# A decoder's expert weights leave one by one behind named cross-attention products instead of in one go

## What is computed

```python
x = _layernorm(x + _L1_attn_ref(x, w_qkv, w_o))
x = _layernorm(x + _L1_xattn_ref(x, ctx_2048, ctx_2048))
logits = x @ gate_w.T
topk_w, topk_idx = top_k(softmax(logits), 8)
for e in range(64):           # w13: 256x256, w2: 256x128 per expert
    h = silu(x @ w13[e, :128].T) * (x @ w13[e, 128:].T)
    acc += combine[:, e:e+1] * (h @ w2[e].T)
x = _layernorm(x + acc)
```

## Time and profile before

| | us |
|---|---|
| runs of the kernel | 808.4, 811.34, 811.78 (median 811.34) |
| profiled execution | 814.26 |
| its span | 812.9 |
| PE busy | 736.4 (91%) |
| DVE busy | 496.7 (61%) |
| POOL busy | 371.7 (46%) |
| ACT busy | 369.5 (45%) |

### The profile page before, as it was taken

How to read it: one execution, slowest core, us unless ns; L and a number is a source line. 1 busy time by engine, 2 the same in 40 slices (tenths; PEclk the granted TensorE clock), 3 DMA queues, 4 the chain that set the end, 5 groups by cost and what they waited for, 6 DMA issues and landing times.

```text
span 812.9 us, 17140 instructions
## 1 busy us (share of the span) xinstructions
PE 736.4 (91%) x5723; PEld 607.9 (75%) x5723; DVE 496.7 (61%) x1520; ACT 369.5 (45%) x962; POOL 371.7 (46%) x488
## 2 busy tenths in 40 slices
PE   8999999999999999999999777749988899888975
PEld 6667877878787888888777554338887787888854
DVE  4887878666657665877688665425454445434335
ACT  3465546443555566667776333412222222344325
POOL 1142221233734444435687544563555555555535
PEclk9999999999999999999999998959999999999998
DMA  9465430011356554333464389247768898633266
GB/s 241 108 213 180 136 109 8 1 40 44 102 131 204 173 172 137 111 112 87 150 172 123 86 310 344 83 135 262 226 196 269 270 291 291 197 116 96 82 235 251
DMA packets 95598, 132.00 MB, mean 162 GB/s; under 512 B 29511, under 2 KB 65905, under 8 KB 95256
## 3 DMA queue, kind: packets, MB, share of 16 engines
q1 hardware_dynamic: 86344, 113.57, 45.8%
q0 software_dynamic: 9168, 17.35, 5.8%
HBM read 116.29 MB, written 35.58 MB: 187 GB/s over the span
## 4 chain that ended last, share of the span: by engine, by line
PE 64%; DVE 7%; issue 6%; another core or an unknown queue 6%; DMA 6%; POOL 4%; ACT 4%; SPq 3%; DVEq 0%; POOLq 0%; ACTq 0%
PE ps L214 58%; PE ps L217 6%; DMA rows_e<-x_slots 1%; POOL x_slots L1639 1%; SPq L1261 1%; ACT soft L585 1%; DMA rowso<-y_slots 1%; DMA y_slots<-o_e,index_e 1%; DMA wh<-in_wqkv 1%; POOL w_lo L1131 1%; ACT pTc L1477 1%; DVE topc L1527 1%; DMA w_sb<-in_w 1%; POOL y_slots L2034 1%
## 5 line engine op out<-in xcount | busy, mean ns | idle before, releaser
L2034 POOL DMA_INDIRECT y_slots<-o_e,index_e x127 | 124.4, 980 | 111.8 <-DVE o_e L2025 72.6
L1131 POOL TENSOR_TENSOR w_lo<-wh,w_hi 128x256 fp32r<-128x256 f32 x120 | 91.6, 771 | 101.6 <-ACT w_hi L1005 100.0
L214 PE MATMUL ps<-xT_e,w_slot 128*128 128x128 f32 x760 | 99.2, 280 | 7.4 <-issue 7.0
L2015 DVE TENSOR_TENSOR h_e<-ps,gate_e 128x256 f32<-128x256 f32 x64 | 26.9, 421 | 120.2 <-ACT gate_e L1962 91.3
L214 PEld LDWEIGHTS ps<-xT_e,w_slot 128*128 128x128 f32 x760 | 92.0, 195 | 10.6 <-issue 9.9
L1639 POOL DMA_INDIRECT x_slots<-rows_all,index_all x64 | 62.7, 979 | 23.9 <-issue 17.7
L1956 ACT COPY xT_e<-ps 128x512 f32<-128x512 f32 x64 | 37.1, 580 | 72.8 <-PE ps L217 28.5
L214 PE MATMUL ps<-x_hi,w_hi 128*128 128x512 f32 (+1 forms) x240 | 69.9, 372 | 0.1
L1962 ACT ACTIVATE gate_e<-ps 128x256 f32<-128x256 f32 x64 | 24.6, 384 | 96.7 <-PE ps L214 49.0
L1005 ACT CAST w_hi<-wh 128x256 fp32r<-128x256 f32 x120 | 47.8, 407 | 41.2 <-PE ps L214 37.5
L214 PE MATMUL ps<-x_lo,w_hi 128*128 128x512 f32 (+1 forms) x240 | 64.1, 349 | 0.0
(11 more groups left out here) (288 smaller groups left out, 1734.6 us busy)
## 6 DMA issues: line engine op xcount, KB each, us to landing
w_slot<-in_we SPq DMA_DIRECT2D x95, 384.0 KB
rows_e<-x_slots SPq DMA_DIRECT2D x127, 136.0 KB
wh<-in_wqkv SPq DMA_DIRECT2D x40, 384.0 KB, 3.2
x_slots<-blank SPq DMA_DIRECT2D x4, 2176.0 KB, 9.5
w_kept<-in_we SPq DMA_DIRECT2D x20, 384.0 KB
sums<-key_sums SPq DMA_DIRECT2D x24, 256.0 KB
wo<-in_wo SPq DMA_DIRECT2D x40, 128.0 KB
rowso<-y_slots SPq DMA_DIRECT2D x10, 512.0 KB, 7.6
```

Of the source, the lines that this page charges most:

```text
L214: return self.pe.matmul(out, lhsT, rhs, start=start, stop=stop, skip_group_check=shared)
L1131: pool.tensor_tensor(t.w_lo[n % 2][:, :, which, :], t.wh[n % 2][:, :, which, :], t.w_hi[n % 2][:, :, which, :], ALU.subtract).then_inc(*t. ...
L2015: dve.tensor_tensor(T.h[:, 0:n, :].rearrange("p s t -> p (s t)"), ExpertBanks(m, p - 1).up[:, 2 * P:(2 + n) * P], T.gate[:, 0:n, :].rearra ...
L2034: pool.indirect_dma_start(m.y_slots, bass.IndirectOffsetOnAxis(ap=T.index[:, s:s + 1], axis=0), T.o[:, s, :], None, bounds_check=TOK * TOP ...
```

## The change

The loads of the first 8 slot weights move from `sp_experts` into lane k, ahead of the kept weights, and lane k (now `sp_later_weights`) waits before load n for the TensorE product that `WEIGHT_PACE` names for it. The numbers of the table are (product, sequence). Lane k has 28 steps, and the context of sequence 7 stands behind five of them instead of 14.

```diff
+WEIGHT_PACE = {
+    1: ("turned 0", 4), 2: ("turned 0", 4), 3: ("values 0", 4), 4: ("values 0", 4), 5: ("values 1", 4),
+    6: ("scores 1", 5), 7: ("scores 0", 6), 8: ("tops", 5), 9: ("back", 4), 10: ("turned 0", 5),
+    11: ("turned 0", 5), 12: ("values 0", 5), 13: ("scores 1", 6), 14: ("values 1", 5), 15: ("scores 0", 7),
+    16: ("tops", 6), 17: ("back", 5), 18: ("turned 0", 6), 19: ("rank", 5), 20: ("scores 1", 7),
+    21: ("values 0", 6), 22: ("values 1", 6), 23: ("tops", 7), 24: ("turned 0", 7), 25: ("back", 6),
+    26: ("turned 1", 7), 27: ("rank", 6),
+}
...
+    def done_on_pe(self, name, b):
+        part = int(name[-1]) if name[-1].isdigit() else 0
+        return {"scores": lambda: self.s_ps(2 * b + part + 1), "tops": lambda: self.topT_ps(b + 1), "turned": lambda: self.sT_ps(2 * b + part + 1),
+                "values": lambda: self.v_ps(2 * b + part + 1), "columns": lambda: self.avT_ps(b + 1), "back": lambda: self.back_ps(b + 1),
+                "rank": lambda: self.rank_ps(b + 1)}[name.split()[0]]()
...
-def sp_kept_weights(m, a, t, t1):
+def sp_later_weights(m, a, t, t1, tc):
+
+    def paced(n):
+        if n in WEIGHT_PACE:
+            m.sp.wait_ge(*tc.done_on_pe(*WEIGHT_PACE[n]))
+
     after_attention1(m.sp, t1)
+    for n in range(SLOTS):
+        paced(n)
+        load_weights(t, m.sp, LOADS[n], own_weights(a, LOADS[n]))
+        yield
     for e in range(EARLY, KEPT):
+        paced(SLOTS + e - EARLY)
         m.sp.dma_start(t.kept[e][:, :], a["we"][e, :, :]).then_inc(*t.kept_in.one)
         yield
...
-    for n in range(SLOTS):
-        load_weights(t, sp, LOADS[n], own_weights(a, LOADS[n]))
     for j in range(WORK):
```

## The result

| | before | after |
|---|---|---|
| median of 19 runs each | 812.2 us (803.04 to 819.25) | 817.44 us (809.43 to 825.11) |
| after over before | | 1.0075, 95% interval 1.0049 to 1.0102 |
| profiled execution, its span | 814.26, 812.9 us | 810.49, 809.2 us |

The account below looks back on a forecast made before the run. It took the chain of hand-overs between TensorE, VectorE and ScalarE, then GpSimd's scatters, as the bound, not bandwidth. 7:rank's -2.6 us and one scatter's +1.27 gave -1.3, from 811.34 to 810.0 us; range 804.5 to 816.0.

Parts of the forecast that it names:

- GpSimd's wait of 1.55 us for it goes: On GpSimd, 5:norm5 no longer stands behind two VectorE maxima; its 1.55 us wait goes, worth 0 at the end.
- every product keeps its place against the scatters of the sequences before it: TensorE products beside GpSimd's scatters: reason for taking hand-over delays as unchanged, sum -1.3 us.
- 6:back or 7:tops 3.79 us in place of 1.40, for +1.1: Hand-overs of TensorE results: if either meets the longer delay, the sum becomes +1.1 us instead of -1.3.
- Sequence 7 is ahead, as forecast: End of the routing chain: 7:values1 and 7:rank gain 2.6 us, 7:rank moving from 533.01 to 530.4 us.
- The twelfth scatter: GpSimd behind the root of sequence 7: 12 scatters instead of 11, one more costing 1.27 us.
- 7:scores0 ahead of 5:columns: TensorE order: covered by 1.12 us idle against a 1.15 us product; without the cover, 1.1 us.
- The fill and the clock: TensorE: one fill pair less lies in a wait; a lower granted clock might cost 0.9 us a product; taken as 0.
- The weights: SP's 28 weight loads, paced behind TensorE products: later loads and first uses cost 0, freed bandwidth gains 0.
- The faster rival: Weights cause the long hand-over delays; pacing gives 5.2 us more, 804.9 us; chance 0.21.
- The slower rival: Paced weights beside scatters up to 520 us lengthen later hand-overs: 814.8 us, with a third 817.2; chance 0.16.
- the paces do nothing: SP's weight loads: named products are always done, weights leave in one go, only orders count; 810.0 us, chance 0.06.
- No weight came late: Rival at the experts: weights landing behind 545.4 us cost one us each, 815 at 4 us; chance 0.03.

Follow-up runs that it names:

- norm5_early: The kernel before with one VectorE step moved, 5:norm5 ahead of 7:top0 and 7:top1; ratio to the kernel before 1.0056.
- one_break: The changed kernel with one wait added: GpSimd waits for 6:values1 ahead of scatter 5:sc2; ratio to the kernel before 0.9931.
- after_again: The changed kernel itself, nothing altered, traced and timed a second time; ratio to the kernel before 1.0062.
- old_pool_order: The changed kernel with only GpSimd's order (ORDER_POOL) taken from the kernel before; ratio to the kernel before 1.0030.
- old_orders_paced: Engine orders and banks of the kernel before, with the changed kernel's weight loads, slots first and paced; ratio to the kernel before 1.0040.
- kept_behind_rank7: The changed kernel with the 8 slot weights in one go and all 20 kept weights held until 7:rank; ratio to the kernel before 1.0246.
- no_pace: The changed kernel with WEIGHT_PACE emptied, so weights leave without waiting for products; ratio to the kernel before 1.0050.
- paced_both: The kernel before with scatters 3:sc1 to 6:sc5 each waiting for a TensorE product, and weights paced, slots first; ratio to the kernel before 0.9841.
- scatters_held: The changed kernel with scatters 5:sc0 to 6:sc4 moved behind 7:root5 on GpSimd; ratio to the kernel before 1.0103.

## Why the prediction was wrong

**The step that failed.** "GpSimd's wait of 1.55 us for it goes. GpSimd then waits longer for the next root, so this is worth 0 at the end." The wait goes, and GpSimd does wait longer for the next root (9.15 us at 529.02); the 0 is wrong. That wait had been the only break in GpSimd's series. Behind it, early in the new series of six, 7:scores1 and 6:values1 were handed over within 0.2 and 1.4 us of their modelled ends (511.41 and 512.41 us); in norm5_early, late in a series of eight, it took 4.0 and 5.9 us (from 510.65 and 511.64). I costed the wait as time on GpSimd's queue and not as what it gave to other engines. norm5_early removes it alone and loses 1.9 to 9.4 parts in a thousand; one_break puts one back and wins more than the loss.

**The step that rested on it.** That "every product keeps its place against the scatters of the sequences before it" was my reason for carrying the delays over unchanged. It does not: the scatters moved too. I had allowed 6:back or 7:tops 3.79 us in place of 1.40, for +1.1; the product that was hit was 6:values1, at 7.58 us. With that, 6:rank comes 8.2 us later in the stretch, where I had it about 0.5 us earlier.

**What was right in the orders.** Sequence 7 is ahead, as forecast: from 6:rank to 7:rank it takes 7.8 us (528.67 to 536.51) in place of 13.0. That is 5.2 us given back of the 8.2, and it leaves +3.0 at 7:rank (+2.3 in after_again) where I had -2.6. The twelfth scatter costs what it was sized at: the last one starts 15.96 us behind 7:rank in place of 14.70, 1.26 us more. At tile 7 the stretch is 3.5 us longer, 3.8 in after_again.

**7:scores0 ahead of 5:columns**, "covered", 0.2 to 0.4 us: wrong in size. TensorE did have the time: 5:columns starts at 498.02 us, 24.3 behind 3:rank, as before (497.67, 24.4). But 5:back, at 503.29, waited 3.56 us, the chain has 3.10 and 2.03 us of late hand-overs there, and 5:rank comes 2.7 to 3.9 us later than before. These results fall into a series of seven scatters in place of six. With six (old_pool_order) 5:rank is 2.0 us late, with 5:columns first and seven scatters 4.3 us (0.8 of it at 4:rank already). How the rest divides was not settled.

**The fill and the clock**, taken at 0. A window of the changed kernel (columns as in the earlier trace rows):

```profile
518.00:531.00 13.00, 8.40 (x83) 5.13 (x84) 4.79 (x19) 4.74 (x6) 3.17 (x4) 0.74 0.69 213
```

The granted clock of 518 to 531 us is 0.74 in place of 0.91, and 7:turned0 at 523.16 us took 2.09 us, against 1.15 for 7:turned1 at 526.59: about 0.9 us. It goes with the wait of 5.32 us and not with the missing fill, for in one_break, with the same fills, the clock of the same window is 1.00. So it is part of the price of the late hand-over.

**The weights**, 0 and 0: held. old_orders_paced moves no step in the table by over 0.3 us, and nobody waits for a weight. So the choice that the delays come from the scatters was right. The faster rival (804.9 us) is out: the piece of 3.79 us, which pacing was to bring down to 1.40, is 3.84 us in old_orders_paced and 3.76 in the changed kernel, and kept_behind_rank7 has the longest wait without a weight in flight.

**The slower rival** gave 814.8 to 817.2 us, and the median, 817.44 us, landed at its upper end, but that was luck: its mechanism, weights beside the scatters, is not the one, since no_pace and kept_behind_rank7 have the long delay without weights. The condition of "the paces do nothing" did not come, for the weights left one by one; that the orders alone decide, as it had it, is what no_pace shows, at a time that it had wrong. No weight came late.

**What stays open.** The stretch accounts for 3.5 to 3.8 us of the 4.0 to 8.3. The rest can't be read from single traces: from the turn of tile 7 (558.13 and 563.49 us) to the end of the span the same changed kernel took 251.1 us in one trace and 256.4 in the other, the kernel before 258.7. Nor is it tied to paced weights. old_orders_paced is 3.3 us longer in time (0.4% of 818.29) and 0.3 us in its stretch, but one_break and paced_both, with paced weights too, are shorter in time by 5.6 and 12.9 us and in their stretch by 4.4 and 9.3. Whether pacing weights costs anything by itself was not shown either way.

## What to carry to other kernels

When a change takes away a wait, ask not only what the waiting engine gains but what the pause let through on others; here a GpSimd wait of 1.55 us that looked like pure loss saved ScalarE over 5 us of waiting. Where an engine issues a series of indirect DMAs beside a chain of short steps on other engines, break the series where the chain needs a result: here one semaphore wait ahead of a scatter more than won back the loss. And a piece booked to an unknown releaser is to be explained before its size is carried over to a new order, because it moves with whatever causes it.

## What the runs showed of the hardware

While GpSimd issues indirect DMAs of some 0.96 us with gaps of 0.30 us, an engine that waits for a TensorE product can wake late, by 6.9 us behind the series of eight in the changed kernel (521.41 against 514.51 us), and a pause of 1.17 us between two scatters lets the result through at once (one_break). The longest waits end 1.2 to 1.7 us behind the last scatter of their series: 503.41 behind 502.17 us in the kernel before, 521.41 behind 519.88 in the changed one, 517.53 behind 515.95 in norm5_early, 524.66 behind 522.98 in kept_behind_rank7. In scatters_held, without scatters from 510.84 to 528.56 us, no wait of that stretch is booked to an unknown releaser. The weights' DMA traffic is not needed for it: with q0 alone it is as large.

What about the scatters does it stays open. The rows that they move land at the same time: in windows of 0.2 us, q0's last data moved until 517.0 us in norm5_early and until 524.0 in kept_behind_rank7, 0.5 and 0.7 us ahead of the two wakes. No run has GpSimd's issuing without q0's transfers, or the other way round.

The Trainium skill, page "TensorE: Matmul & The Clock Gate", section "The cost: per-tile semaphore tail", says that semaphore increments of matmuls are written one after the other and gives some 26 ns for each. No run here shows that price by itself. In the changed kernel the results of 6:values1 and 7:tops reach ScalarE and VectorE 0.09 us apart (521.41 and 521.50 us), in turn, but 6.9 and 4.7 us behind their modelled ends (514.51 and 516.82), so a tail of some 26 ns for each is not what they wait for. The page "Perfetto Trace Analysis" of the Trainium skill, section "Tensor Engine Instruction (MATMUL, LD_WEIGHTS)", says that the end of a matmul in a profile is an estimate, and lists the acknowledgement and the signal of its result behind that end. The trace of the changed kernel fits it: the row of 7:tops starts at 515.98 us, behind 6:values1 and 5.4 us before ScalarE wakes for 6:values1. That speaks for a signal that was held up, but these runs don't prove it against a product that itself ended late; they show that the waiter wakes late, and that the scatters decide it.
